# First four x tiles quantised as bytes over preset fp16 words; scale folded into the Newton step; gate matmuls issued in eighths; new instruction orders

## What is computed

```python
def fake_quant(x, scale, zp):
    q = jnp.clip(jnp.round(x / s + z), 0.0, 255.0)
    return (q - z) * s
x = x + matmul(fake_quant(layernorm(x), s1, z1), fake_quant(ctx, s2, z2))   # per batch
h = layernorm(x)
gate_logits = h @ gate_w.T                       # 8 experts, top 2, softmax weights
result = h @ base_w.T + base_b
low = einsum('bsd,erd->ebsr', h, lora_A)         # 8 experts x rank 16 = 128 columns
result = result + 2.0 * einsum('ebsr,eor,bse->bso', low, lora_B, w_full)
x = x + result
```

## Time and profile before

| | before |
|---|---|
| median of 3 runs | 172.59 us |
| profiled execution, first to last instruction | 171.0 us |
| TensorE (PE) busy | 161.2 us, 94% |
| VectorE (DVE) busy | 120.0 us, 70% |
| ScalarE (ACT) busy | 89.9 us, 53% |
| GpSimd (POOL) busy | 16.4 us, 10% |
| granted TensorE clock | 1.000 in the whole span |
| DMA | 32.69 MB |

### The profile page before, as it was taken

How to read it: one execution, slowest core, us unless ns; L and a number is a source line. 1 busy time by engine, 2 the same in 40 slices (tenths; PEclk the granted TensorE clock), 3 DMA queues, 4 the chain that set the end, 5 groups by cost and what they waited for, 6 DMA issues and landing times.

```text
span 171.0 us, 2357 instructions
## 1 busy us (share of the span) xinstructions
PE 161.2 (94%) x801; PEld 118.3 (69%) x801; DVE 120.0 (70%) x309; ACT 89.9 (53%) x140; POOL 16.4 (10%) x33
## 2 busy tenths in 40 slices
PE   5976699999999999999999999999999999999992
PEld 1323244578888888876888764876888888888881
DVE  0698799999999999977887698963286245505203
ACT  3188797856990588516157274415955708700000
POOL 3030212000020300022200030004004000000000
PEclk9999999999999999999999999999999999999999
DMA  3999999949999699364895609652993996200303
GB/s 81 390 385 421 370 383 357 249 84 362 403 394 283 150 242 305 70 108 78 153 276 111 77 11 201 115 103 53 199 122 46 202 238 254 94 29 2 123 0 123
DMA packets 22187, 32.69 MB, mean 191 GB/s; under 512 B 13856, under 2 KB 13856, under 8 KB 22176
## 3 DMA queue, kind: packets, MB, share of 16 engines
q1 hardware_dynamic: 20016, 25.20, 46.1%
q0 software_dynamic: 2016, 7.34, 23.2%
q10 hardware_dynamic: 144, 0.00, 0.0%
HBM read 22.05 MB, written 4.19 MB: 154 GB/s over the span
## 4 chain that ended last, share of the span: by engine, by line
PE 83%; DMA 8%; DVE 3%; SPq 2%; issue 1%; ACT 1%
PE ps_odd L1031 26%; PE ps_even L1031 26%; PE ps_att L977 10%; PE ps_g L1013 6%; DMA ring<-in_ctx 5%; DMA x_sb<-in_x 3%; PE ps_g L1016 2%; PE ps_even L977 2%; PE ps_t L958 2%; PE ps_even L1074 1%; PE ps_odd L1074 1%; PE ps_odd L1072 1%; PE ps_even L1073 1%; PE ps_odd L1073 1%; PE ps_even L1072 1%
## 5 line engine op out<-in xcount | busy, mean ns | idle before, releaser
L1031 PE MATMUL ps_even<-w_hi,yt 128*128 128x512 f32 x128 | 36.6, 395 | 0.0
L1031 PE MATMUL ps_odd<-w_hi,yt 128*128 128x512 f32 x128 | 36.4, 402 | 0.0
L1031 PEld LDWEIGHTS ps_odd<-w_hi,yt 128*128 128x128 f32 x128 | 23.6, 188 | 5.2
L1031 PEld LDWEIGHTS ps_even<-w_hi,yt 128*128 128x128 f32 x128 | 23.7, 188 | 5.1
L977 PE MATMUL ps_att<-c,c1t 128*128 128x512 f16 x96 | 23.0, 379 | 0.2 <-ACT c1t L420 0.2
L1031 PE MATMUL ps_even<-w_lo,yt 128*128 128x512 f32 x64 | 20.1, 392 | 0.0
L1031 PE MATMUL ps_odd<-w_lo,yt 128*128 128x512 f32 x64 | 18.8, 391 | 0.0
L1013 PE MATMUL ps_g<-ag,yt 128*128 128x272 f32 x64 | 16.5, 332 | 0.0
L977 PEld LDWEIGHTS ps_att<-c,c1t 128*128 128x128 f16 x96 | 8.8, 98 | 10.9 <-issue 1.8
L630 DVE BATCH_NORM_STATS2 stats<-x_sb 128x6 f32<-128x512 f32 x16 | 11.0, 686 | 5.1 <-DMA x_sb<-in_x 4.9
L408 ACT ACTIVATE qc<-ring,q_in,q_rec 128x1024 uint16<-128x1024 f32 x11 | 13.4, 1232 | 1.8 <-issue 1.0
(11 more groups left out here) (108 smaller groups left out, 251.4 us busy)
## 6 DMA issues: line engine op xcount, KB each, us to landing
ring<-in_ctx SPq DMA_DIRECT2D x12, 512.0 KB, 9.4
w_raw<-in_w_t SPq DMA_DIRECT2D x8, 512.0 KB, 7.0
x_sb<-in_base_b POOLq DMA_DIRECT2D x8, 512.0 KB, 6.4
out_x<-x_sb SPq DMA_DIRECT2D x16, 256.0 KB, 2.6
x_sb<-in_x SPq DMA_DIRECT2D x7, 512.0 KB, 5.3
x_sb<-zfix POOLq DMA_DIRECT2D x6, 512.0 KB, 5.9
x_sb<-in_ctx SPq DMA_DIRECT2D x4, 512.0 KB, 5.6
ag_raw<-in_ag_t SPq DMA_DIRECT2D x1, 544.0 KB, 7.6
```

Source lines behind the costliest of these rows:

```text
L1031: pe.matmul(ffn_bank[t % 2][h][:, :], rows_of(part, t, k), w[:, k, h * HALF:(h + 1) * HALF], start=start, stop=False)
```

## The change

1. x tiles 0 to 3 are quantised in one pass. VectorE's `byte_ones(t)` sets the whole fp16 tile c1[t] to 1024.0 beforehand; the quantised value is then written as uint8 into the low byte of each word, which makes the word 1024 + q. ScalarE's `scale_x` does so for tiles 1 to 3, VectorE's `quantise_x(0)` for tile 0. `cut_x` is left for tiles 4 to 7 alone. The constant 1024 + 128 is taken off where c1t leaves PSUM (`take_c1t`) and in `zero_point_row`.
2. The factor 1/s1 goes into the square root: ScalarE's Ln takes s1^2 as its scale and eps s1^2 as its bias, and the Newton step works on that, so `x_constants(t)` has four instructions.
3. The products of scales go from VectorE (`quant_constants`, four instructions) to GpSimd (`square_constants`, four, and `quant_constants`, three).
4. `low_and_gate(t, k)` is a call per k, put between attention and base calls.
5. All five lists get a new order. SP: x(3) comes after context 6, W 0 to 2 after context 8, W 3 to 7 before x(4), and x(4) to x(6) before context 11; transposes go ahead of stores. GpSimd: `add_bias(0)` comes before `add_zfix(3)`. TensorE: attention(1, 0..3) comes before attention(0, 5..7), attention(3, ...) is ended before base_high(0, 0), base_high and low_and_gate of tiles 0 and 1 are mixed. VectorE: `add_attention(3)`, `variance(0, 4)` and `cut_context` 9 to 15 come later, `variance(1, 1)` earlier.

```diff
-            def quant_constants():
-                dve.wait_ge(q_ready, 1)
...
             def scale_x(t):
                 act.wait_ge(qb_ready, t + 1)
-                if t >= 2:
-                    act.wait_ge(c1_ready, t - 1)
-                act.activation(qx[:, t % 2, :], x_sb[:, t, :], ACT.Relu, bias=qb[:, t:t + 1],
+                if t < TPB:
+                    act.wait_ge(bytes_ready, t + 1)
+                    to = low_bytes(t)
...
+                g = r0[:, 0, t:t + 1]
+                dve.wait_ge(r0_ready[0], t + 1)
+                chain(dve.tensor_scalar(r_v[:, 0, t:t + 1], mv[:, 0, t, 1:2], EPS, g, ALU.add, ALU.mult))
+                chain(dve.tensor_scalar(r_h[:, 0, t:t + 1], r_v[:, 0, t:t + 1], g, q_sq[:, 2:3], ALU.mult, ALU.mult))
+                chain(dve.tensor_scalar(qa[:, t:t + 1], r_h[:, 0, t:t + 1], 1.5, g, ALU.add, ALU.mult))
+                dve.scalar_tensor_tensor(out=qb[:, t:t + 1], in0=mv[:, 0, t, 0:1], scalar=qa[:, t:t + 1],
+                                         in1=q_in[:, 1:2], op0=ALU.mult, op1=ALU.subtract,
+                                         reverse1=True).then_inc(qb_ready, 1)
+
+            def byte_ones(t):
+                dve.memset(c1[:, t, :], BYTE_ONE).then_inc(bytes_ready, 1)
+
+            def quantise_x(t):
+                dve.wait_ge(qb_ready, t + 1)
+                dve.wait_ge(bytes_ready, t + 1)
+                dve.tensor_scalar(low_bytes(t), x_sb[:, t, :], qa[:, t:t + 1], qb[:, t:t + 1],
+                                  ALU.mult, ALU.add).then_inc(qx_ready[t], 1)
...
+            def low_and_gate(t, k):
...
+            for k in range(0, 4):
+                base_high(0, k)
+            for k in range(0, 5):
+                low_and_gate(0, k)
+            base_high(0, 4)
...
+            base(2, 3)
+            low_and_gate(2, 1)
+            attention(4, 0)
+            low_and_gate(2, 2)
+            attention(4, 1)
```

More of the change, by code:

```diff
@@ L18 @@
 QMAX = 255.0
+BYTE_ONE = 1024.0
 EPS = 1e-5
@@ L786, in finish_tile @@
                                              op0=ALU.add, op1=ALU.add).then_inc(out_ready, 1)
[L788 to L795, removed]
+            for k in range(0, 3):
+                byte_ones(k)
+            quant_reciprocals()
+            variance(0, 0)
+            x_constants(0)
+            quantise_x(0)
             variance(0, 1)
@@ L873, in _ @@
             cut_x(5)
+            variance(0, 6)
+            split_low_lo(2)
+            split_y_lo(3, 1)
             add_attention(4)
@@ L1128, in _ @@
[L1128 to L1131 removed]
+            for k in range(0, 4):
[3 more added lines that the diff above has]
+            base_high(0, 4)
+            transpose_y(1, 0)
+            low_and_gate(0, 5)
+            low_and_gate(0, 6)
+            base_high(0, 5)
+            base_high(0, 6)
+            low_and_gate(0, 7)
+            transpose_y(1, 1)
@@ new lines, in _ @@
+            base_high(0, 7)
+            base_low(0, 0)
+            for k in range(0, 3):
+                low_and_gate(1, k)
+            base_high(1, 0)
+            for k in range(3, 6):
+                low_and_gate(1, k)
+            base_high(1, 1)
+            base_high(1, 2)
+            low_and_gate(1, 6)
+            low_and_gate(1, 7)
+            base_high(1, 3)
+            base_low(0, 1)
+            base_low(0, 2)
+            transpose_y(2, 0)
+            base_high(1, 4)
+            transpose_low(0)
@@ L1170, in _ @@
+            attention(5, 4)
+            low_and_gate(3, 6)
+            attention(5, 5)
+            low_and_gate(3, 7)
+            attention(5, 6)
             lora(2, 0)
             lora(2, 1)
-            attention(5, 3)
+            attention(5, 7)
+            base(3, 6)
             transpose_low(3)
-            for k in range(4, 8):
-                attention(5, k)
             base(3, 7)
@@ L1186, in _ @@
+            attention(7, 2)
+            low_and_gate(4, 4)
+            attention(7, 3)
+            low_and_gate(4, 5)
+            attention(7, 4)
+            low_and_gate(4, 6)
+            attention(7, 5)
             base(4, 3)
-            base(4, 4)
+            low_and_gate(4, 7)
+            for k in range(4, 7):
+                base(4, k)
             transpose_low(4)
-            for k in range(4, 8):
-                attention(7, k)
-            for k in range(5, 8):
-                base(4, k)
+            attention(7, 6)
@@ L1193, in _ @@
+            base(4, 7)
+            low_and_gate(5, 0)
+            low_and_gate(5, 1)
+            attention(7, 7)
+            for k in range(2, 8):
+                low_and_gate(5, k)
             lora(4, 0)
+            base(5, 0)
+            base(5, 1)
             lora(4, 1)
-            low_and_gate(5)
-            for k in range(0, 5):
+            base(5, 2)
+            base(5, 3)
+            transpose_low(5)
+            for k in range(4, 7):
                 base(5, k)
-            transpose_low(5)
@@ new lines, in _ @@
+            base(7, 0, (0,))
+            base(7, 1, (0,))
+            transpose_low(6)
+            base(6, 4)
+            for k in range(0, 3):
+                low_and_gate(7, k)
+            base(7, 0, (1,))
+            for k in range(3, 7):
+                low_and_gate(7, k)
+            base(7, 1, (1,))
+            low_and_gate(7, 7)
+            base(7, 2, (0,))
+            base(7, 2, (1,))
+            base(6, 5)
+            base(7, 3, (1,))
+            transpose_low(7)
+            base(7, 4, (1,))
```

487 lines of the change are left out of this document (248 added, 239 removed).

## The result

The changed kernel takes 176.43 us (median of 4 runs, 174.58 to 178.93) where the kernel before takes 172.5. I had forecast 169.7 us. The profiled execution has a span of 173.5 us (its own time is 175.72).

A forecast was written before the change was run, and what follows sets the result against it. PE was taken to bound the kernel after a front short of work. Span 171.0 - 2.5 (front) + 0.65 (handover) - 1.1 (eighths) = 168.05, plus 1.6 around it: 169.65, say 169.7 us; range 168.7 to 172.0.

The forecast's parts named there:

- Other edits: Late loads of x(4) and contexts 11 to 15 behind the reordered GpSimd additions: no loss, some 4 us of room.
- rival 3: W tiles land too late for PE's base matmuls; PE stands 5.8 us, time 175.4 us; chance 0.08.
- rival 1: VectorE sets the pace from y(0) on, so PE's lead shrinks to 0.7 us; time 170.8 us; chance 0.17.
- 0.08 for slower: Chance given to a measurably slower kernel, all of it from W weights coming too late.
- The front: Start of the kernel up to the transposes of c1(2): PE would be 2.5 us ahead by earlier contexts and single-pass quantising.
- The loss of 0.65 us: Handover to the feed-forward at base_high(0, 0): PE waits for y(0), ready at 30.0 us, and its split, losing 0.65 us.
- The bound of 0.4 us: Strided byte writes in scale_x(1) to (3): at most 0.2 us extra each, 0.4 in all before zfix; lower bound nothing.
- the bounds 0.42 and 1.22: VectorE's memset in byte_ones was put between 0.42 and 1.22 us a call, with no loss to the sum.
- The eighths: low_and_gate pairs with attention behind them hide a stationary-operand load: 20 pairs at 0.053 us, 1.1 us gained.
- rival 2: Splitting low_and_gate into calls between attention matmuls gains nothing; time 170.7 us; chance 0.12.
- rival 4: Small waits from thin margins add up to 2 to 3 us over tiles 0 to 5; time 172.2 us; chance 0.08.
- The sum: Whole kernel: span 168.05 us plus 1.6 for what lies around it, 169.65, said as 169.7 us.

The follow-up runs named there:

- a_load: Changed kernel with SyncE loading contexts 11 and 12 right after W 7, before x(4) to x(6): 170.74 us, on a second chip 170.64.
- a_exp: Changed kernel with exp_gate(1) moved ahead of scale_context(11) and (12) on ScalarE: 175.27 us.
- a_warm: Changed kernel with 18 unused matmuls on ones put before transpose_low(1), where PE stood idle: 174.78 us.
- a_two: a_load2 with x tiles 1 to 3 quantised in two passes again: 170.93 us against 169.82 for a_load2 on the same chip.
- b_ops: Kernel before with the new operations (bytes, folded scale, products on GpSimd) in the old lists, gate in blocks: 173.32 us, ratio 1.005.
- a_load2: a_load with the load of lora_B moved from before ag to after W 7: 170.10 us, on another chip 169.82.

## Why the prediction failed, step by step

- **The step that failed** is the part "Other edits", which put the late loads at "No loss, with some 4 us of room". It followed the queue rightly as far as the first load (add_zfix(3) behind add_bias(0) behind W 7, x(4) asked for at 47.5; measured 48.5). Then it went wrong twice. It asked when attention(4, ...) needs the contexts, at 70 us; but who waits first is the call that stands at the head of ScalarE's list: scale_context(11) at 53 us, with exp_gate(1) and the y split of tile 2 behind it, which PE wants at 61.7. And it had contexts 11 to 13 land by 56 us, six tiles at 1.3 to 1.4 us each, with no share for the bias additions 2 and 1 in the same stretch, at its own 2.8 us each; contexts 11, 12 and 13 landed at 58.1, 61.9 and 64.1.
- **Both slips were needed for the stall.** From the landing of context 12 to transpose_low(1) it is 2.8 us, and PE wants that at 61.7, so a landing by 58.9 us would have cost nothing; at the 1.28 us between x(4) and x(5) context 12 would have landed at 53.2 + 3 x 1.28 = 57.0. These two are estimates from the changed kernel's trace. That moving the two loads removes the whole loss is shown by a_load; that the queue and not one call in it is the link, by a_exp; that the stall would also go if only the additions moved is argued, not shown.
- **Rivals 3 and 1** didn't happen in the changed kernel. W 7 had landed when GpSimd went on at 40.6 us (forecast 39.6 to 41.7), and no wait of PE for a weight is listed. None of the rivals was this mechanism, so 0.08 for slower was too little: I had given each queue one consumer, and counted no chance for one that I had looked at and passed.
- **The clock** was in no sum. I had treated each us of wait as one us of time; the 3.0 us stall was followed by 1.8 us of clock loss (a_warm), of which about 1.0 shows in the span, because the rest covers the wait at attention(4, 0).
- **The front** was right. Its timeline in the changed kernel, with the three marks that the prediction set:

```profile
20.34 0.61 PE L974 MATMUL ps_t<-ident_h,c 128*128 128x128 f16 x8
...
24.75 1.46 PE L1002 MATMUL ps_even<-c,c1t 128*128 128x512 f16 x6
...
29.46 0.81 DVE L745 TENSOR_SCALAR y<-x_sb,mv,rstd 128x1024 f32<-128x1024 f32 x1
```

  Expected: transposes of c1(2) at 20.5 us, measured 20.34 against 25.19; zfix scaled to 24.6, attention(2, 0) at 24.85, measured 24.75; first base matmul 33.24 instead of 34.13, with six more attention matmuls (1.3 us) done by then. The lead at that point is so 0.89 + 1.30 = 2.2 us, where the prediction had 2.5 - 0.65 = 1.85. That it depends both on the bytes (1.1 us, a_two) and on the order of loads and calls (b_ops without it) is more than the prediction said; it gave all 2.5 us to the two together.
- **y(0)** was written at 29.46 + 0.81 = 30.3, forecast 30.0, before 30.7. The loss of 0.65 us at base_high(0, 0) was not there: PE's first base matmul began 0.48 us after its last attention matmul, so only 0.26 us late. ag had landed at 29.3 us, where I had put 31.5, and ScalarE was done with it at 31.04, before the transpose of y was there to split.
- **Byte writes and memsets,** in the same timeline:

```profile
2.10 0.91 DVE L693 MEMSET c<- 128x1024 f16 x1 [0.16 <-issue]
...
3.17 0.91 DVE L693 MEMSET c<- 128x1024 f16 x1 [0.16 <-issue]
...
8.08 0.82 DVE L698 TENSOR_SCALAR c<-x_sb,qa,qb 128x1024 uint8<-128x1024 f32 x1
...
13.84 1.23 ACT L453 ACTIVATE c<-x_sb,qb,qa 128x1024 uint8<-128x1024 f32 x1
```

  Bytes cost what int16 cost: 1.23 us on ScalarE and 0.82 on VectorE. The bound of 0.4 us from strided 16-bit writes wasn't used up. The memset took 0.91 us, 1.07 from start to start; of the bounds 0.42 and 1.22 I had let the upper stand. By the Trainium skill (VectorE: DVE Perf Modes, Zero memsets can be issued as uint32) a memset takes one cycle per element whatever the type; my estimate from it, at the page's 0.96 GHz, was 1.07 us, and the trace agrees.
- **The eighths** have the right mechanism and the wrong size and count: 0.04 us a pair, not 0.053. And 21 pairs have attention behind them, not 20 (seven in tile 3), while in the kernel before the last pairs of tiles 3 and 4 had it already, so 19 are won: 19 x 0.04 = 0.8 us, not 1.1. A second pair of traces agrees. From the first base matmul to the last start the kernel before takes 133.23 us; without the six attention matmuls that the new list does earlier, 131.93; a_load2 takes 131.15, 0.78 less, with the same calls. So rival 2 is false, and rivals 1 and 4 with it, since a_load2 has no wait of PE behind 33 us in the view. I took the gap in the block to go wholly; the pair between attention matmuls still takes 0.20 us, where its 408 columns at the pace of attention, 0.217 us for 512, would take 0.17. By the Trainium skill (TensorE: Matmul & The Clock Gate, LDWEIGHTS) the load of a stationary operand takes its columns divided by 1.2, in ns; for 128 columns my estimate from it is 107 ns. In the block of rows 8 the loads of the 4-byte operands begin 0.11 to 0.13 us apart, so the trace agrees, and two of them make up the 0.24 us of a pair; each record itself lasts 0.19 us.
- **The sum.** 1.6 us around the span was the difference between a profiled span of 171.0 and the median of other runs. Taken run by run it is 1.9 us before and 2.2 after the change. With 168.05 + 2.2 = 170.3, the prediction's sum without the stall stands against 170.7 for a_load and 170.0 for a_load2 (the middle of its two medians): the wrong sign came from one queue. That the sum fits so well is in part luck: the eighths gave 0.3 us less than forecast and the front 0.35 more, and the two cancel.

## What to carry to other kernels

When a load is delayed, its first user isn't the computation that needs the data but the first call in any in-order list that waits for it; look at what stands behind that call, all of it, since here two calls were late one after the other. When you lay out the landing times, count every transfer of the stretch, also those that another engine issues. A queue in which one wait stands ahead of transfers that don't need it is cured by moving the transfers, here at no cost; moving a late call out from behind the block only showed the next. A stall of TensorE can cost more than its length: here 3.0 us without work were followed by 1.8 us of clock loss.

## What the runs showed that I had not expected

The granted clock fell to 0.50 after 3.0 us without PE work and was 0.65 over the next stretch; after the 2.8 us of a_exp it was 0.71, 0.50 and 0.93 in the three stretches from 64 to 70 us. With the gap filled (a_warm) it stayed at 1.000. The time outside the span of instructions was 1.8 to 2.1 us in the runs of the kernel before and 2.1 to 2.3 in the kernels with the new operations; no view shows what fills these 0.3 us, and it stays open. A program that writes bytes into the lower halves of 16-bit words, every second byte, paid nothing for the stride on either engine (0.82 and 1.23 us for 1024, as for int16 side by side).
